# A two-layer graph kernel: the masked attention product in one VectorE instruction from PSUM, and the neighbour maximum in two strided reductions

## The chip, the cores and the metric

The program runs on one core of a Trainium2 chip. The metric is device time in microseconds (us). Three executions of the kernel before gave 5440.72, 5489.24 and 5507.57 us; the median is 5489.24 us. The profile is of one execution, whose span is 5448.3 us.

## The reference, cut to what matters

There are 8 graphs of 2048 nodes with 256 features. Layer 0 takes, for each node, the first 25 neighbours in column order, gathers their 256 features and keeps the maximum per feature; a product with a 512 x 256 matrix, a residual and a layer norm follow. Layer 1 is an attention with 4 heads of 64 features, over the same adjacency matrix.

```python
# layer 0: neighbour maximum
vals, idx = jax.lax.top_k(jnp.where(A != 0, pri, neg_inf), S)       # S = 25, pri = -column
feats = jax.vmap(lambda x, i: x[i])(X, idx)                         # gather 25 rows
agg = jnp.where(valid[..., None], feats, neg_inf).max(axis=2)
out = relu(concat([X, agg]) @ W + b);  x = layernorm(x + out)
# layer 1: attention over the nonzero entries (all are of type 1)
weight = leaky_relu(e_src[i] + e_dst[j], 0.01); weight = where(adj == 0, NEG, weight)
dst = softmax(weight) @ h + bias;  out = per_head_norm(relu(dst) + h);  x = layernorm(x + out)
```

With one edge type, exp(leaky_relu(s + d)) is a factor of i and a factor of j times max(r_i * q_j, 1), where r = exp(0.99 s) and q = exp(0.99 d). The kernel computes that, masks it, and divides by the sum.

## The kernel before, in words

The 16384 nodes are 128 tiles of 128 rows; four tiles are a quad, and `run_quads` unrolls the four steps u = 0 to 3 of a quad. One step works on several tiles at once, each at another stage. Every engine has its own `step` function, and the program order in it is written by hand; engines meet at semaphores.

In step s (= 4q + u) the engines do this:

- **GpSimd (POOL)** gathers the neighbours of tile s: 25 indirect DMAs (L498), one per neighbour slot, each 128 rows of 256 floats into `rows`. It waits for the index list `idx` of that tile, and per chunk of 5 slots until VectorE has read the chunk's old content.
- **VectorE (DVE)** runs the search for tile s+1 in `step`: a chain of 35 links (`LINKS`), each waiting for the one before: the words of the mask (L728, L729), `top32` three times (L715, L717), and the list `idx` at its end (L768). Between the links stands other work at numbered places: the masked units of attention at `UNIT_AT` (and one ahead of the chain, one at the step's end), the residual and norm of tile s-1 at 7 to 17 (L778 at place 7 needs TensorE's product `p_lin`), the maxima of the gathered chunks at 12, 19 and 26 (L836). After the chain come the last maximum, `aggregate` (L845 reduces 5 x 256 to 256, L846 clips and signals `s_agg`), and the last masked unit. In steps with u = 0, `divide` stands at place 6; the rest of a finished quad (`finish_*`) lies in u = 1 to 3.
- **ScalarE (ACT)** makes r*q for each unit (`scaled`, L565: two 128x512 Copy activations with a per-partition scale, from the tile `rb` in SBUF), the mask conversions (L517 to L546), the projection's exponentials (L653 to L663), and the copy of the attention sums out of PSUM (L586).
- **TensorE (PE)** multiplies each masked unit into the accumulators (`attend`, L1231), and does the products and transposes of the two layers. At a step's end it waits for `s_agg`, transposes (L1186), runs `attend` for unit 7, and in the next step comes `back` (u = 0 only) and `product0` (L1199, L1200), which signals `s_lin`.
- **SyncE** issues the plain DMAs. The values r go to DRAM and come back broadcast over 128 partitions into `rb` (1 MB a quad).

Attention of tile block m runs 16 steps behind. A unit is one tile of neighbours j (128) with two heads: before, a step handles 4 neighbour tiles and all four heads, in 8 units. VectorE's unit is one instruction over 2 x 512 elements: max(uv, 1) * mask, both inputs in SBUF (L819). There are four `uv` buffers.

## Time and profile before

| what | value |
|---|---|
| device time, median of 3 (lowest, highest) | 5489.24 us (5440.72, 5507.57) |
| span of the profiled execution | 5448.3 us |
| busy PE / DVE / ACT / POOL | 63% / 76% / 57% / 68% |
| granted TensorE clock, mean | 0.78 of full speed |

For the profiled execution the page gives its span alone, and not the device time around it. Busy shares are means over a start of 16 steps without attention, some 112 steps with everything, and a tail of attention alone. An engine's busy time leaves out the time between its instructions.

### The profile page before, as it was taken

Reading aid. Unit: us, or ns where it says so; the run is one execution under the profiler, and the core shown is the slowest. Engines: PE = TensorE matmul, PEld = TensorE weight load, DVE = VectorE, ACT = ScalarE, POOL = GpSimd, SP = SyncE. Lnnn points to the kernel's source line nnn. Section 1 sums busy time; section 2 is a strip of 40 time slices with the busy share of each in tenths; the row PEclk is TensorE's granted clock in tenths of the full one; section 3 lists DMA queues with packets and bytes.
Section 4 is the critical chain, followed back from the end, with each engine's and each line's share of the span. In section 5 each row is a group of like instructions: output and inputs, shape, how many; then the busy total and the mean of one; then the engine's idle time right before and its main releaser. Section 6 shows DMA issues by size and latency. Waiting matters only on the chain.

```text
span 5448.3 us, 58256 instructions
## 1 busy us (share of the span) xinstructions
PE 3438.2 (63%) x11778; PEld 1438.1 (26%) x11778; DVE 4138.1 (76%) x11484; ACT 3111.4 (57%) x5570; POOL 3717.1 (68%) x3204
## 2 busy tenths in 40 slices
PE   1232467666666767666676666666666666666786
PEld 1121222222222222222222222222222222222222
DVE  4555578878787888878787878888878788787777
ACT  3333456666556666656655655656656666555565
POOL 4666777777777777777777777777777777677400
PEclk9555578777778777878777787787888778778798
DMA  3434344444444444444444444444444444444210
GB/s 113 130 119 136 119 138 128 146 132 146 125 129 133 135 144 135 132 143 129 134 133 133 145 125 127 139 130 146 136 144 131 128 139 131 137 131 133 85 39 27
DMA packets 282021, 692.71 MB, mean 127 GB/s; under 512 B 62849, under 2 KB 130178, under 8 KB 265346
## 3 DMA queue, kind: packets, MB, share of 16 engines
q0 software_dynamic: 153600, 419.64, 26.1%
q1 hardware_dynamic: 128130, 270.41, 15.6%
q14 instruction: 257, 2.11, 0.1%
q8 instruction: 34, 0.56, 0.0%
HBM read 639.21 MB, written 50.59 MB: 127 GB/s over the span
## 4 chain that ended last, share of the span: by engine, by line
POOL 36%; issue 25%; DVE 22%; PE 8%; DMA 4%; ACT 3%; another core or an unknown queue 1%; POOLq 0%; DVEq 0%; SPq 0%; ACTq 0%
POOL rows L498 36%; PE acc L1231 5%; DVE uv L819 5%; DVE rmax L836 4%; DMA rows<-in_x_dram,idx 4%; DVE top L715 2%; DVE key_b L717 1%; PE pB L1199 1%; DVE agg L845 1%; DVE sth L892 1%; ACT uv L565 1%; DVE key_a L717 1%; DVE mvh L898 1%; ACT stage L525 0%
## 5 line engine op out<-in xcount | busy, mean ns | idle before, releaser
L498 POOL DMA_INDIRECT rows<-in_x_dram,idx x3200 | 3716.9, 1162 | 1404.5 <-issue 997.0
L1231 PE MATMUL acc<-uv,hs 128*65 128x512 f32 x4096 | 2301.4, 712 | 707.2 <-DVE uv L819 448.3
L565 ACT ACTIVATE uv<-rb,qj 128x512 f32 (+1 forms) x2048 | 1330.4, 712 | 169.6 <-PE acc L1231 137.6
L819 DVE SCALAR_TENSOR_TENSOR uv<-uv,maskT 128x1024 f32<-128x1024 f32 x1024 | 1239.9, 1221 | 183.6 <-ACT uv L565 148.4
L1231 PEld LDWEIGHTS acc<-uv,hs 128*65 128x65 f32 x4096 | 602.6, 160 | 1992.7 <-issue 1403.4
L836 DVE TENSOR_TENSOR rmax<-rmax,rows 128x1280 f32<-128x1280 f32 x384 | 572.5, 1491 | 600.4 <-DMA rows<-in_x_dram,idx 553.5
L628 ACT ACTIVATE xaT<-pA 128x512 f32<-128x512 f32 x128 | 76.4, 597 | 791.3 <-PE pA L1186 610.6
L542 ACT ACTIVATE stage<-pT 128x1024 bf16<-128x1024 f16 x256 | 260.6, 1018 | 288.8 <-remote 148.0
L1186 PE MATMUL pA<-id,xt 128*128 128x128 f32 x256 | 81.5, 419 | 469.4 <-DVE agg L846 334.2
L640 ACT ACTIVATE x1T<-pA 128x256 f32<-128x256 f32 x128 | 49.2, 384 | 570.8 <-PE pA L1209 394.5
L1199 PE MATMUL pB<-w_sb,xaT 128*128 128x256 f32 x1024 | 348.0, 499 | 18.4 <-ACT xaT L628 8.6
L836 DVE TENSOR_TENSOR rmax<-rows 128x1280 f32<-128x1280 f32 x128 | 191.5, 1496 | 172.6 <-DMA rows<-in_x_dram,idx 172.6
L1199 PEld LDWEIGHTS pB<-w_sb,xaT 128*128 128x128 f32 x1024 | 257.0, 262 | 170.6 <-DVE pad L730 87.6
L845 DVE TENSOR_REDUCE agg<-rmax 128x256 f32<-128x1280 f32 x128 | 297.2, 2322 | 4.4
L1209 PE MATMUL pA<-id,xh 128*128 128x128 f32 x256 | 63.2, 334 | 366.1 <-DVE xh L810 341.5
L546 ACT ACTIVATE maskT<-pT 128x1024 f16 (+1 forms) x256 | 260.5, 1018 | 0.0
L1215 PE MATMUL pB<-wcat,x1T 128*128 128x264 f32 x512 | 205.6, 539 | 81.5 <-ACT x1T L640 63.9
L525 ACT ACTIVATE stage<-adj_sb,minus 128x2048 bf16<-128x2048 int32 x128 | 254.1, 1985 | 0.0
L517 ACT ACTIVATE mask_sb<-adj_sb 128x2048 f16<-128x2048 int32 x128 | 243.0, 1898 | 2.0 <-DMA adj_sb<-in_adj_dram 2.0
L715 DVE MAX8 top<-key_a 128x8 f32<-128x104 f32 (+1 forms) x768 | 209.9, 273 | 34.7 <-DVE key_a L717 10.1
L715 DVE MAX8 top<-key_b 128x8 f32<-128x104 f32 (+1 forms) x768 | 207.5, 270 | 35.5 <-remote 20.6
L1160 PE MATMUL pB<-pack,stage 128*128 128x8 bf16 x2048 | 75.3, 169 | 222.6 <-ACT stage L542 221.2
(113 smaller groups left out, 3755.5 us busy)
## 6 DMA issues: line engine op xcount, KB each, us to landing
adj_sb<-in_adj_dram SPq DMA_DIRECT2D x128, 1024.0 KB
rows<-in_x_dram,idx POOLq DMA_INDIRECT x3200
xh_dram<-xh SPq DMA_DIRECT2D x128, 256.0 KB
rb<-r_dram SPq DMA_DIRECT2D x32, 1024.0 KB
xr<-xh_dram SPq DMA_DIRECT2D x64, 512.0 KB
xt<-in_x_dram SPq DMA_DIRECT2D x128, 128.0 KB
out_dram<-xr SPq DMA_DIRECT2D x32, 512.0 KB
r_dram<-er SPq DMA_DIRECT2D x128, 2.0 KB
```

The source lines that it names most:

```text
L498: nc.gpsimd.indirect_dma_start(rows[:, c, r * C:(r + 1) * C], None, x_rows, bass.IndirectOffsetOnAxis(ap=idx[p][:, k:k + 1], axis=0)).then ...
L517: nc.scalar.activation(mask_sb[:], adj_sb[:], ACT.Sign, accum_out=degree[:, bass.ds(g, 1)]).then_inc(s_mask, 1)
L525: nc.scalar.activation(stage[:].rearrange("p j i -> p (j i)"), adj_sb[:], ACT.Square, scale=2.0, bias=minus1[:], accum_out=adj_sq[:, bass. ...
L542: nc.scalar.activation(stage[:, hf * HALF:(hf + 1) * HALF, :], src, ACT.Square).then_inc(s_stage, 1)
L546: nc.scalar.activation(maskT[:, bass.ds(qg % RING * JT + hf * HALF, HALF), ug * P:(ug + 1) * P], src, ACT.Square).then_inc(s_ring, 1)
L565: last = nc.scalar.activation(uv[k][:, i, :], rb[:, bass.ds(qa % 2, 1), h, :].rearrange("p a i -> p (a i)"), ACT.Copy, scale=q_j(h))
L715: ch.then(nc.vector.max(top[:, k:k + 8], a))
L819: nc.vector.scalar_tensor_tensor(uv[k][:], uv[k][:], 1.0, m, ALU.max, ALU.mult).then_inc(s_u, 1)
L836: nc.vector.tensor_tensor(rmax[:], before, rows[:, c, :], ALU.max).then_inc(s_rfree, 2 if c == 1 else 1)
L845: ch.then(nc.vector.tensor_reduce(agg[:], rmax[:].rearrange("p (r f) -> p f r", f=C), axis=AX.X, op=ALU.max))
L1199: nc.tensor.matmul(p_lin, xaT[:, c, :], w0_sb[:, c, :], start=(c == 0), stop=False)
L1231: last = nc.tensor.matmul(acc[h][0:HW, :], hs[:, (1 - quad.par) * JT + jt, h, :], uv[k][:, i, :], start=(jt == 0), stop=(jt == JT - 1))
```

## The change

Attention is reordered within a quad. Heads are handled in pairs: steps u = 0, 1 do heads 0 and 1 over all 16 neighbour tiles, steps u = 2, 3 heads 2 and 3. The product r*q is no longer formed: the factors are rewritten as mask * max(r, 1/q), with 1/q in `qinv` as the per-partition scalar, and q moved into `hs`. The row r is broadcast over the partitions by TensorE (`broadcast`: two matmuls of `er` with a 0/1 selector, 128x512 each, into the PSUM tiles `rq`), once for each pair, so twice a quad. VectorE then makes each half unit with one instruction over 512 elements, `rq` in PSUM as its first input and the mask in SBUF as its second: 16 a step in place of 8 of 1024. ScalarE's `scaled` goes away, with `r_dram`, `rb` and their DMAs.

Two accumulators in place of four serve a pair, so their hand-over (`numerators` on ScalarE, `back` on TensorE, `divide` on VectorE) happens twice a quad, at u = 0 and at u = 2.

The 25 gathered rows are read in two chunks of 13 and 12 slots. Each chunk is one `tensor_reduce` over a view whose inner dimension steps over the slots (stride 256 floats), at place 19 and at the end of the chain, and `aggregate` joins the two halves with one `tensor_tensor`.

```diff
@@ -44,14 +44,15 @@
 WPT = P // WORD
 NIB = 4
 TOP = 32
-CH = 5
-CR = S // CH
+CH = 2
+SLOTS = (0, 13, S)
 FIRST = S + 1
 HALF = JT // 2
 UNITS = JT * 2
 US = UNITS // QT
+PAIR = 2
+HJ = JT // 2
 UVB = 4
-AHEAD = 3
...
-        rows = sb("rows", [P, CH, CR * C], F32)
-        rmax = sb("rmax", [P, CR * C], F32)
+        rows = sb("rows", [P, S * C], F32)
+        rmax = sb("rmax", [P, CH, C], F32)
...
-        qj = sb("qj", [P, 2 * JT, HEADS], F32)
+        qinv = sb("qinv", [P, 2 * JT, HEADS], F32)
         dj = sb("dj", [P, HEADS], F32)
         wide = sb("wide", [P, HEADS + 1], F32)
-        er = [sb(f"er{p}", [HEADS, P], F32) for p in range(2)]
-        rb = sb("rb", [P, 2, HEADS, IB], F32)
-        uv = [sb(f"uv{k}", [P, 2, IB], F32) for k in range(UVB)]
-        sT = sb("sT", [HW, HEADS, IB], F32)
+        er = sb("er", [P, 2 * N], F32)
+        headsel = sb("headsel", [HEADS, HEADS, P], F32)
+        uv = [sb(f"uv{k}", [P, PAIR, IB], F32) for k in range(UVB)]
+        sT = sb("sT", [HW, PAIR, IB], F32)
+        raw = sb("raw", [P, QT, C], F32)
...
-        acc = [ps(f"acc{i}", [P, 512], F32) for i in range(QT)]
+        acc = [ps(f"acc{i}", [P, 512], F32) for i in range(PAIR)]
+        rq = [ps(f"rq{i}", [P, IB], F32) for i in range(PAIR)]
...
-                    sp.dma_start(r_dram[:, bass.ds((s - 2) * P, P)], er[p][:]).then_inc(s_rst[p], 16)
-                if u == 1 and quad.on(u, QT * BQ - QT):
-                    m = quad.q - BQ + 1
-                    for o in range(2):
-                        for v in quad.reach(lambda q: 32 * (q - BQ + 2)):
-                            sp.wait_ge(s_rst[o], v)
-                            sp.sem_inc(s_go["sp"], 1)
-                    for v in quad.reach(lambda q: UNITS * (q - BQ)):
-                        sp.wait_ge(s_v, v)
-                        sp.sem_inc(s_go["sp"], 1)
-                    dst_rb = rb[:, bass.ds(m % 2, 1), :, :].rearrange("p a h i -> p (a h) i")
-                    src_rb = r_dram[:, bass.ds(m * IB, IB)].partition_broadcast(P)
-                    sp.dma_start(dst_rb, src_rb).then_inc(s_rb, 16)
...
-                    for r in range(CR):
-                        k = c * CR + r
+                    for k in range(SLOTS[c], SLOTS[c + 1]):
                         nc.gpsimd.indirect_dma_start(
-                            rows[:, c, r * C:(r + 1) * C], None, x_rows,
+                            rows[:, k * C:(k + 1) * C], None, x_rows,
...
-                last.then_inc(s_v, 1)
-            def scaled_units(quad, u, a, b):
-                if quad.on(u, QT * BQ):
-                    for n in range(a, b):
-                        scaled(quad, u, n)
+                for v in quad.reach(lambda q: 2 * (q - lag) + pair):
+                    act.wait_ge(s_back, v)
+                for i in range(PAIR):
+                    last = nc.scalar.activation(sT[:, i, :], acc[i][0:HW, :], ACT.Identity, bias=tiny[0:HW, :])
+                last.then_inc(s_sT, 1)
...
-                nc.scalar.activation(dj[:], p_ed, ACT.Exp, scale=LEAK).then_inc(s_ed, 1)
-                nc.scalar.activation(qj[:, bass.ds(t, 1), :], p_ed.unsqueeze(1), ACT.Exp, scale=1.0 - LEAK)
-                nc.scalar.activation(er[p][:], p_es, ACT.Exp, scale=1.0 - LEAK, accum_out=r_sum[:, bass.ds(QT * qg + ug, 1)])
+                nc.scalar.activation(dj[:], p_ed, ACT.Exp).then_inc(s_ed, 1)
+                nc.scalar.activation(qinv[:, bass.ds(t, 1), :], p_ed.unsqueeze(1), ACT.Exp, scale=LEAK - 1.0)
+                nc.scalar.activation(er[0:HEADS, bass.ds(t * P, P)], p_es, ACT.Exp, scale=1.0 - LEAK,
+                                     accum_out=r_sum[:, bass.ds(QT * qg + ug, 1)])
...
-            def masked(quad, u, n):
-                jt, k = QT * u + n // 2, n % UVB
-                for v in quad.reach(lambda q: UNITS * (q - BQ) + US * u + n + 1):
-                    dve.wait_ge(s_v, v)
-                m = maskT[:, bass.ds((quad.q - BQ) % RING * JT + jt, 1), :].to_broadcast([P, 2, IB])
-                nc.vector.scalar_tensor_tensor(uv[k][:], uv[k][:], 1.0, m, ALU.max, ALU.mult).then_inc(s_u, 1)
-                if u == QT - 1 and n == US - 1:
-                    nc.vector.memset(tick[:, 4:5], 0.0).then_inc(s_blk, 1)
+            def masked(quad, u, n, i):
+                pair, jt, k = u // 2, HJ * (u % 2) + n, n % UVB
+                h = PAIR * pair + i
+                if i == 0:
+                    for v in quad.reach(lambda q: UNITS * (q - BQ) + US * u + n - UVB + 1):
+                        dve.wait_ge(s_pe, v)
+                    if n == 0:
+                        dve.wait_ge(s_proj, projected(quad, u))
+                        if u % 2 == 0:
+                            for v in quad.reach(lambda q: 2 * (q - BQ) + pair + 1):
+                                dve.wait_ge(s_rq, v)
+                m = maskT[:, bass.ds((quad.q - BQ) % RING * JT + jt, 1), :].rearrange("p a i -> p (a i)")
+                inv = qinv[:, (1 - quad.par) * JT + jt, h:h + 1]
+                stt = nc.vector.scalar_tensor_tensor(uv[k][:, i, :], rq[i][:], inv, m, ALU.max, ALU.mult)
+                if i == PAIR - 1:
+                    stt.then_inc(s_u, 1)
+                    if u == QT - 1 and n == US - 1:
+                        nc.vector.memset(tick[:, 4:5], 0.0).then_inc(s_blk, 1)
             def maximum(quad, u, c):
-                if c == 1:
-                    for v in quad.reach(lambda q: 16 * CR * (QT * q + u + 1)):
-                        dve.wait_ge(s_rows[0], v)
-                else:
-                    for v in quad.reach(lambda q: CH * (QT * q + u + 1) + c):
-                        dve.wait_ge(s_rfree, v)
-                for v in quad.reach(lambda q: 16 * CR * (QT * q + u + 1)):
+                count = SLOTS[c + 1] - SLOTS[c]
+                for v in quad.reach(lambda q: 16 * count * (QT * q + u + 1)):
                     dve.wait_ge(s_rows[c], v)
-                before = rows[:, 0, :] if c == 1 else rmax[:]
-                nc.vector.tensor_tensor(rmax[:], before, rows[:, c, :], ALU.max).then_inc(s_rfree, 2 if c == 1 else 1)
+                slots = rows[:, SLOTS[c] * C:SLOTS[c + 1] * C].rearrange("p (s f) -> p f s", f=C)
+                nc.vector.tensor_reduce(rmax[:, c, :], slots, axis=AX.X, op=ALU.max).then_inc(s_rfree, 1)
             def aggregate(quad, u):
@@ -842,26 +795,27 @@
                 for v in quad.reach(lambda q: QT * q + u):
                     dve.wait_ge(s_xaT, v)
                 ch = Chain(dve, s_maxc)
-                ch.then(nc.vector.tensor_reduce(agg[:], rmax[:].rearrange("p (r f) -> p f r", f=C), axis=AX.X, op=ALU.max))
+                ch.then(nc.vector.tensor_tensor(agg[:], rmax[:, 0, :], rmax[:, 1, :], ALU.max))
                 nc.vector.tensor_scalar(agg[:], agg[:], lim[u % 2][:, 0:1], lim[u % 2][:, 1:2], ALU.max, ALU.min).then_inc(s_agg, 1)
                 ch.end()
-            def divide(quad):
-                for v in quad.reach(lambda q: q - BQ):
+            def divide(quad, pair):
...
+                        dve.wait_ge(s_out, v)
+                    nc.vector.tensor_tensor(dst[:], raw[:], per_column(bias_b), ALU.add).then_inc(s_fin, 1)
...
-            UNIT_AT = (2, 4, 6, 14, 22, 31)
-            CHUNK_AT = (12, 19, 26)
+            UNIT_AT = (3, 4, 5, 6, 9, 13, 14, 18, 21, 22, 23, 25, 28, 30, 31, 33)
+            CHUNK_AT = 19
...
-                        masked(quad, u, 1 + UNIT_AT.index(place))
+                        masked(quad, u, UNIT_AT.index(place) // PAIR, UNIT_AT.index(place) % PAIR)
                     if behind and place in RESIDUAL_AT:
                         residual(quad, u, RESIDUAL_AT.index(place))
                     if fin and u == 0 and place == DIVIDE_AT:
-                        divide(quad)
+                        divide(quad, 1)
+                    if att and u == 2 and place == DIVIDE_AT:
+                        divide(quad, 0)
                     if behind and place in NORM_AT:
                         norm0(quad, u, NORM_AT.index(place))
-                    if gather and place in CHUNK_AT:
-                        maximum(quad, u, 1 + CHUNK_AT.index(place))
+                    if gather and place == CHUNK_AT:
+                        maximum(quad, u, 0)
...
+            def broadcast(quad, pair):
+                for v in quad.reach(lambda q: UNITS * (q - BQ) + pair * UNITS // 2):
+                    pe.wait_ge(s_u, v)
+                    pe.sem_inc(s_go["pe"], 1)
+                block = (quad.q - BQ) % BQ * IB
+                for i in range(PAIR):
+                    last = nc.tensor.matmul(rq[i][:], headsel[:, PAIR * pair + i, :],
+                                            er[0:HEADS, bass.ds((1 - quad.par) * N + block, IB)], start=True, stop=True)
+                last.then_inc(s_rq, 1)
...
             def step(quad, u):
+                if quad.on(u, QT * BQ):
+                    pe.wait_ge(s_proj, projected(quad, u))
+                    if u % 2 == 0:
+                        broadcast(quad, u // 2)
                 if u == 0 and quad.on(u, FIN):
-                    back(quad)
+                    back(quad, 1)
+                if u == 2 and quad.on(u, QT * BQ):
+                    back(quad, 0)
                 if quad.on(u, 1):
                     product0(quad, u)
-                if quad.on(u, QT * BQ):
-                    if u == 0:
-                        for v in quad.reach(lambda q: q - BQ):
-                            pe.wait_ge(s_accfree, v)
-                    pe.wait_ge(s_proj, projected(quad, u))
+                if quad.on(u, QT * BQ) and u % 2 == 0:
+                    for v in quad.reach(lambda q: 2 * (q - BQ) + u // 2):
+                        pe.wait_ge(s_accfree, v)
                 attend(quad, u, 0, 4)
```

TensorE's order at a step's start moves as follows. These rows are of the kernel before, from the unit that follows the transposes of `agg` at the end of step u = 1 to the first units of step u = 2.

```order
L1186 MATMUL pA<-id,agg 128x128 x2
L1228 REGISTER_ALU
L1231 MATMUL acc<-uv,hs 65x512 x2
L1199 MATMUL pB<-w_sb,xaT 128x256 x4
L1200 MATMUL pB<-b_sb,ones_row 128x256
L1228 REGISTER_ALU
L1231 MATMUL acc<-uv,hs 65x512 x2
```

The same place in the changed kernel:

```order
L1155 MATMUL pA<-id,agg 128x128 x2
L1197 REGISTER_ALU
L1200 MATMUL acc<-uv,hs 65x512 x2
L1138 MATMUL rq<-er,headsel 128x512 x2
L1123 REGISTER_ALU
L1127 MATMUL acc<-id,sT 128x65 x8
L1168 MATMUL pB<-w_sb,xaT 128x256 x4
L1169 MATMUL pB<-b_sb,ones_row 128x256
```

The broadcast and eight transposes now stand between the last unit of a pair and the product that signals `s_lin`.

VectorE in the changed kernel, in step u = 1, from the first masked half unit (place 3 of the chain) to the residual at place 7:

```order
L777 SCALAR_TENSOR_TENSOR uv<-rq,qinv,maskT 128x512
L666 MATCH_REPLACE key_b<-top,key_a 128x128
L777 SCALAR_TENSOR_TENSOR uv<-rq,qinv,maskT 128x512
L664 MAX top<-key_b 128x8
L768 REGISTER_ALU
L777 ISA
L777 SCALAR_TENSOR_TENSOR uv<-rq,qinv,maskT 128x512
L666 MATCH_REPLACE key_a<-top,key_b 128x128
L777 SCALAR_TENSOR_TENSOR uv<-rq,qinv,maskT 128x512
L664 MAX top<-key_a 128x8
L727 SCALAR_TENSOR_TENSOR r<-pB,xt 128x256
```

Between `agg` and this residual there now lie these four half units; before, five whole units lay there (unit 7 of the step that ends, unit 0, and units 1 to 3 at places 2, 4 and 6).

## Rows read from the trace of the kernel before

**Rows 1.** Windows: busy us (instructions) per engine, granted TensorE clock, DMA share, GB/s.
```profile
200.00:600.00 400.00, 127.28 (x592) 80.27 (x593) 208.69 (x691) 142.21 (x275) 270.77 (x266) 0.55 0.41 126
1200.00:4800.00 3600.00, 2419.47 (x8261) 998.05 (x8262) 2885.28 (x8038) 2177.51 (x3912) 2661.96 (x2245) 0.79 0.44 134
```

**Rows 2.** Waits: engine, line, whom it waited for; total us, times, longest.
```profile
DVE rmax L836 <- DMA rows<-in_x_dram,idx: 726.1, 339, 11.1
...
POOL rows L498 <- DVE idx L768: 407.5, 84, 43.0
...
DVE uv L819 <- ACT uv L565: 148.4, 154, 6.5
```

**Rows 3.** Timeline at a step's end: start, length, engine, line, operation [idle before].
```profile
2405.32 1.49 DVE L836 TENSOR_TENSOR rmax<-rmax,rows 128x1280 f32<-128x1280 f32 x1 [1.40 <-DMA rows<-in_x_dram,idx]
2406.07 1.56 POOL L498 DMA_INDIRECT rows<-in_x_dram,idx  x1 [0.30 <-issue]
2406.84 2.31 DVE L845 TENSOR_REDUCE agg<-rmax 128x256 f32<-128x1280 f32 x1
2407.93 0.95 POOL L498 DMA_INDIRECT rows<-in_x_dram,idx  x1 [0.30 <-issue]
```

**Rows 4.** Groups by form: busy us, mean ns of one, idle before and releaser.
```profile
L498 POOL DMA_INDIRECT rows<-in_x_dram,idx x3200 | 3716.9, 1162 | 1404.5 <-issue 997.0 <-DVE idx L768 407.5
...
L819 DVE SCALAR_TENSOR_TENSOR uv<-uv,maskT 128x1024 f32<-128x1024 f32 x1024 | 1239.9, 1221 | 183.6 <-ACT uv L565 148.4 <-issue 33.6 <-DVE dst L926 0.6
...
L836 DVE TENSOR_TENSOR rmax<-rmax,rows 128x1280 f32<-128x1280 f32 x384 | 572.5, 1491 | 600.4 <-DMA rows<-in_x_dram,idx 553.5 <-issue 45.2
...
L845 DVE TENSOR_REDUCE agg<-rmax 128x256 f32<-128x1280 f32 x128 | 297.2, 2322 | 4.4
...
L586 ACT ACTIVATE sT<-acc,tiny 65x512 f32<-65x512 f32 x128 | 77.1, 679 | 25.0 <-PE acc L1231 20.9 <-issue 3.9
...
L778 DVE SCALAR_TENSOR_TENSOR r<-pB,xt 128x256 f32<-128x256 f32 x128 | 52.9, 414 | 97.7 <-PE pB L1200 56.6 <-issue 20.6 <-remote 20.1
L846 DVE TENSOR_SCALAR agg<-agg,lim 128x256 f32<-128x256 f32 x128 | 52.7, 412 | 4.7
```

**Rows 5.** Line L705, the start's four reductions: shortest, median, longest ns.
```profile
L705 DVE TENSOR_REDUCE wcat<-r x4: 419/420/421, 18.4 to 21.2; 128x4 f32<-128x256 f32 x4
```

**Rows 6.** Timeline of VectorE, links of the search with a masked unit between.
```profile
2459.42 0.28 DVE L717 MATCH_REPLACE8 key_b<-top,key_a 128x128 f32<-128x128 f32 x1
2459.61 1.22 DVE L819 SCALAR_TENSOR_TENSOR uv<-uv,maskT 128x1024 f32<-128x1024 f32 x1
2460.75 0.29 DVE L715 MAX8 top<-key_b 128x8 f32<-128x128 f32 x1
2461.07 0.09 DVE L717 MATCH_VALUE_LOAD key_a<-top,key_b 128x8 f32 x1
```

**Rows 7.** Timeline of VectorE and TensorE from the step's end to place 7.
```profile
2454.18 0.41 DVE L846 TENSOR_SCALAR agg<-agg,lim 128x256 f32<-128x256 f32 x1
...
2454.90 0.66 PE L1186 MATMUL pA<-id,xt 128*128 128x128 f32 x2 [9.54 <-issue]
...
2455.78 3.19 PE L1231 MATMUL acc<-uv,hs 128*65 128x512 f32 x4
...
2461.10 0.69 PE L1200 MATMUL pB<-b_sb,ones_row 1*128 1x256 f32 x2
...
2463.05 0.42 DVE L778 SCALAR_TENSOR_TENSOR r<-pB,xt 128x256 f32<-128x256 f32 x1 [0.28 <-PE pB L1200]
```

**Rows 8.** Windows around the same step's end, columns as in Rows 1.
```profile
2450.00:2455.00 5.00, 0.10 (x1) 0.13 (x2) 4.63 (x4) 0.00 (x0) 4.09 (x4) 0.50 0.66 231
...
2460.00:2465.00 5.00, 5.00 (x16) 2.14 (x15) 4.61 (x17) 3.61 (x4) 3.87 (x4) 1.00 0.26 79
```

**Rows 9.** Timeline of TensorE: one unit at either clock.
```profile
2477.58 1.93 PE L1231 MATMUL acc<-uv,hs 128*65 128x512 f32 x4 [0.70 <-issue]
...
2490.63 3.67 PE L1231 MATMUL acc<-uv,hs 128*65 128x512 f32 x4
```

More of the change, by code:

```diff
@@ L298, in layers_program @@
         s_xhst = [sem(f"s_xhst{p}") for p in range(2)]
-        s_rst = [sem(f"s_rst{p}") for p in range(2)]
         s_x1T = sem("s_x1T")
@@ L628, in step @@
                     nc.scalar.activation(xaT[:, :, :], pA[:, :].rearrange("p (c i) -> p c i", c=4), ACT.Copy).then_inc(s_xaE, 1)
-                if next_attends:
-                    for n in range(1, AHEAD):
-                        scaled(quad, u, n, 1)
             def project(quad, u):
@@ L879, in finish_heads @@
                 if part == 0:
-                    nc.vector.tensor_tensor(dst[:], dst[:], per_column(bias_b), ALU.add).then_inc(s_fin, 1)
+                    for v in quad.reach(lambda q: q - BQ - 1):
+                        dve.wait_ge(s_out, v)
+                    nc.vector.tensor_tensor(dst[:], raw[:], per_column(bias_b), ALU.add).then_inc(s_fin, 1)
                 if part == 1:
@@ L1008, in step @@
                     aggregate(quad, u)
-                if att:
-                    masked(quad, u, US - 1)
                 if fin and u == QT - 1:
@@ L1224, in attend @@
                 for n in range(a, b):
-                    jt, hh, k = QT * u + n // 2, n % 2, n % UVB
+                    pair, jt, k = u // 2, HJ * (u % 2) + n, n % UVB
                     for v in quad.reach(lambda q: UNITS * (q - BQ) + US * u + n + 1):
                         pe.wait_ge(s_u, v)
-                    for i in range(2):
-                        h = 2 * hh + i
-                        last = nc.tensor.matmul(acc[h][0:HW, :], hs[:, (1 - quad.par) * JT + jt, h, :], uv[k][:, i, :],
+                    for i in range(PAIR):
+                        h = PAIR * pair + i
+                        last = nc.tensor.matmul(acc[i][0:HW, :], hs[:, (1 - quad.par) * JT + jt, h, :], uv[k][:, i, :],
                                                 start=(jt == 0), stop=(jt == JT - 1))
```

95 lines of the change are left out of this document (33 added, 62 removed).

## The prediction

> **What bounds the kernel now.** I read the windows first, to get the length of a step, then the waits, then the timeline of one step's end. In the middle stretch GpSimd issues 2245 gathers in 3600 us; at 25 a tile that is 89.8 steps of 40.1 us [rows 1]. At the start, without attention, it is 266 gathers in 400 us, or 37.6 us a step. GpSimd alone needs 25 x (1.162 + 0.302 between two) = 36.6 us a step, and 407.5 / 128 = 3.2 us more for the index list [rows 2, 4]. VectorE waits 726.1 / 128 = 5.7 us a step for gathered rows and 148.4 / 112 = 1.3 us for ScalarE [rows 2]; the rest, 40.1 - 5.7 - 1.3 = 33.1 us, is its own chain. So the gathers pace the kernel, closely followed by VectorE, which also holds back the list that the gathers need.
>
> A gather costs 0.95 us when VectorE is in a one-input instruction (the reduction of L845) and 1.56 us when it starts beside a two-input one from SBUF (L836) [rows 3]. The mean of 1.162 [rows 4] is a mixture of the two. The change takes away the two kinds of instruction that do most of this: the masked units and the maxima. GpSimd's step would fall to about 25 x (0.95 + 0.30) + 1.2 for the turn to a new list = 32.5 us. After the change VectorE is therefore the engine to count, and every wait of its own counts in full.
>
> **Masked units.** A unit of 1024 elements lasts 1.22 us but adds less inside the chain: from L717 at 2459.42 to the next link at 2460.75 is 1.33 us, where a link without filler takes its own 0.28 + 0.03, so a unit adds 1.02 [rows 6]; 0.19 us of it overlaps. Six stand there, two outside add some 1.15: 8.4 us a step. A half unit of 512 elements reads PSUM. The nearest row is L778, 256 elements, one input in PSUM, 0.414 us [rows 4]; the slope between L819 and L836 is 0.27 us for 256 elements, so 0.68 us for 512, and 0.49 added. Sixteen make 7.8 us: **-0.6 us a step**.
>
> L778 reads PSUM and takes 414 ns, L846 reads SBUF only and takes 412 [rows 4]: no surcharge shows. The Trainium skill, page "VectorE: DVE Perf Modes", section on the TRN2 errata, gives a fixed part of 120 cycles from PSUM against 58 from SBUF, 65 ns more an instruction; by it sixteen would cost 1.0 us a step more, and the sum would come out 116 us longer. The rows disagree with it here, and I go by the rows.
>
> **The maximum.** Before: three of L836 in the chain at 1.49 - 0.19, one outside at 1.52, L845 at 2.35: 7.8 us a step [rows 4]. After: two reductions over 3328 and 3072 elements and one joint of 256 (0.44, as L846 with its hand-over). Their price is the largest unknown. L845 takes 2.32 us for 1280 elements with an inner step of 1 KB; at the plain 1.05 ns an element and 0.15 us fixed it would be 1.49. L705 shows that plain price, without a stride: 0.42 us for 256 [rows 5]. The surplus of 0.83 us can go two ways. Per element: 1.70 ns each, so 5.8 + 5.4 us. Per output (256, at 3.2 ns): 4.5 + 4.2 us. L705 has 4 outputs and can't tell. Below, the bound is the plain price, 3.6 + 3.4; above, nothing in the trace excludes twice the plain price, 2.1 ns, 7.1 + 6.6. I take the price per element: the stride is what sets L845 apart from L705 and the other instructions, and it is there for each element. So 11.4 in place of 7.8: **+3.6 us a step**; per output it is +1.1.
>
> The Trainium skill, "Advanced Engine Details and Errata", section "SBUF Cachelines", says that accesses which each go to another 16-byte line pay a penalty. L845 agrees with that as far as it goes, since it is slower than its plain price, and this rule speaks against the change.
>
> **Divide.** It happens twice a quad on half the columns: +0.1 us a step (an estimate; a few fixed parts more). VectorE's own chain is then 33.1 - 0.6 + 3.6 + 0.1 = 36.2 us.
>
> **New waits behind the step's end.** VectorE signals `s_agg` at 2454.6; TensorE transposes from 2454.90, runs unit 7 from 2455.78 for 3.19 us, and `s_lin` comes at about 2461.8, 7.3 us or somewhat more after the signal [rows 7]. TensorE is at half clock then: 0.50 before it starts, 1.00 only from 2460 [rows 8]. Before, VectorE filled this time with five units (5.4 us) and 2.4 us of search, and waited 0.28 us at L778. Now it has four half units, 2.0 us, so it arrives after 4.4 us. In steps u = 1 and 3 that is a wait of about 3.2 us at place 7.
>
> At u = 2 the first half unit, at place 3, needs the broadcast, which is queued on TensorE behind the transposes of `agg` and unit 7. These end about 4.6 us after `s_agg`, and two matmul pairs of a unit's size take 1.9 to 3.7 us [rows 9], say 2.7 while the clock rises. The row is there at 7.3, VectorE at 1.1: a wait of 6.2 us. The two copies of ScalarE (L586, 2 x 0.68 [rows 4]) run beside the broadcast; eight transposes and the product follow while VectorE does its half units and the divide, so place 7 adds nothing. At u = 0 `finish_rows`, four instructions of L846's size, covers 1.6 of it: 4.6 us. Mean over a quad: (3.2 + 3.2 + 6.2 + 4.6) / 4 = **4.3 us a step**. The scalar work removed from ScalarE and the DMAs of `rb` had cost the path only the 1.3 us already taken out.
>
> **Sum.** Middle: 36.2 + 4.3 = 40.5 against 40.1 us, x 112 = +45 us. Rows no longer make VectorE wait: the last of 25 gathers is issued 32.5 us after the list and needed at 40. Start: gathers pace it, 37.6 falls to 33.0 (0.5 kept for the small two-input instructions that remain), x 16 = -74 us. Tail: one hand-over more for each of four quads (2 x 0.68 on ScalarE, transposes, divide, some 3.5 us): +14 us. Together -15, so a span of 5433 us. The profiled span, 5448.3, lies 0.7% under the median of 5489.24, and the page gives no device time for this execution; scaled by 1.0075 the forecast is **5475 us**, no change that can be told. About 2% is what a measurement of this kernel can tell from no change.
>
> **Rivals.**
> - *Price per output.* The reductions cost 2.5 us a step less; 38.0 us a step, span 5153, time 5192. For it: L845's groups are short, so a cost for each start of a group is as good a reading. Against it: nothing but the stride. Chance 0.30.
> - *TensorE stays slow after the signal (slower side).* Half units are spread over the step, so TensorE is never long in dense work, and the clock may stay at 0.50 through the unit, the broadcast and the product. A unit then takes 3.67 us, the broadcast 3.7, and the product's second half twice as long [rows 9]: waits grow by 1.9 to 2.4 at odd steps and 1.5 at even ones, 2.0 a step. Span 5433 + 224 = 5657, time 5700. It decides from some 1.1 us a step on, which is half of that. Against it: the same stretch now holds more TensorE work without a gap, and 2460 to 2465 shows it reaching 1.00 after 5 us of work [rows 8]. Chance 0.14.
> - *The reduction costs twice the plain price.* 2.5 us a step more, time up to 5755. Chance 0.08.
> - *The waits don't come.* If TensorE is at full clock when `s_agg` arrives, a unit takes 1.93 us in place of 3.19 [rows 9] and the waits shrink to under 2 us a step: 38.0 a step, about 5190 us. Chance 0.06; the 9.54 us of idle time ahead of these transposes [rows 7] speak against it.
> - *The gathers are not relieved*, because a PSUM input leaves the mask in SBUF. Then GpSimd needs 36.6 + 1.2 us a step, still under 40.5: only the start's 74 us are lost, which stays within the forecast's own range of 5380 to 5590.
>
> The forecast has 0.42. Faster by over 2% (under 5380): 0.30 + 0.04 + a small part of the forecast, 0.36. Slower by over 2% (over 5599): most of the two slow rivals and a little of the forecast, 0.22. Within: 0.42. A range of 5165 to 5650 leaves out the deeper half of the fast cases and the worse half of the slow ones.
>
> **What would show it.** Gathers: mean near 0.97 us, with VectorE waits for rows near zero after the start. Reductions: L789 at 5.8 and 5.4 us (per element), 4.5 and 4.2 (per output). Half units at 0.68 us. New idle time of VectorE ahead of L777 released by TensorE's `rq` matmul, twice a quad, near 6 and 4.6 us, and ahead of the residual near 3 us in odd steps. GpSimd idle, waiting for the list, 7 us a step. The prediction is wrong if the reductions are at the lower price, if the clock behind `s_agg` differs, or if VectorE waits at a place I don't name, such as the free `uv` buffers.

## The result: 30% slower, and the profile after

The changed kernel takes 7097.95 us (median of 4; 7077.05 to 7111.82) against 5472.44 (5440.72 to 5507.57) in the same session: ratio **1.296**, 95% interval 1.288 to 1.304. The forecast was 5475 us, no change that can be told, its range 5165 to 5650. The kernel is clearly slower instead.

First the windows of the changed kernel, of the start and of the middle, columns as in [rows 1]:

```profile
200.00:600.00 400.00, 123.63 (x586) 78.87 (x587) 240.51 (x646) 140.94 (x267) 244.30 (x258) 0.53 0.39 121
1200.00:4800.00 3600.00, 1956.81 (x6118) 765.24 (x6117) 2378.70 (x6373) 935.24 (x1788) 1562.03 (x1629) 0.73 0.31 93
```

1629 gathers are 65.2 steps of 55.2 us, where 40.5 was forecast and 40.1 was measured before [rows 1]. VectorE works 2378.70 / 65.2 = 36.5 us of such a step, GpSimd 24. Neither paces it by its work. The start, without attention, got no faster either: 38.8 us a step, against 37.6 before and a forecast of 33.0.

The groups by form, as in [rows 4], have most of the durations as they were forecast:

```profile
L480 POOL DMA_INDIRECT rows<-in_x_dram,idx x3200 | 3059.9, 956 | 3710.1 <-DVE idx L717 2746.4 <-issue 963.7
...
L777 DVE SCALAR_TENSOR_TENSOR uv<-rq,qinv,maskT 128x512 f32<-128x512 f32 x2048 | 1502.8, 741 | 358.8 <-PE rq L1138 147.6 <-issue 120.6 <-remote 74.5
L789 DVE TENSOR_REDUCE rmax<-rows 128x256 f32<-128x3328 f32 x128 | 739.2, 5775 | 15.9 <-DMA rows<-in_x_dram,idx 15.7
L789 DVE TENSOR_REDUCE rmax<-rows 128x256 f32<-128x3072 f32 x128 | 682.4, 5331 | 3.0 <-DMA rows<-in_x_dram,idx 2.9 <-issue 0.2
...
L727 DVE SCALAR_TENSOR_TENSOR r<-pB,xt 128x256 f32<-128x256 f32 x128 | 54.3, 424 | 918.4 <-remote 732.7 <-issue 103.3 <-PE pB L1169 82.4
```

The reductions cost their price per element, 5.8 and 5.3 us. Gathers fell from 1162 to 956 ns. Rows hardly make VectorE wait: 18.5 us in all, against 726.1 [rows 2]. What is new is the idle time ahead of L727, the residual that needs TensorE's product `p_lin`: 918.4 us in place of 97.7. The waits say more:

```profile
POOL rows L480 <- DVE idx L717: 2746.4, 127, 43.6
...
DVE r L727 <- remote: 732.7, 79, 17.2
...
DVE rden L813 <- remote: 388.4, 40, 16.9
...
DVE top L664 <- remote: 154.8, 98, 3.9
DVE uv L777 <- PE rq L1138: 147.6, 31, 7.6
...
DVE key_a L666 <- remote: 82.0, 42, 2.8
DVE uv L777 <- remote: 74.5, 5, 19.0
DVE key_b L666 <- remote: 60.9, 36, 2.5
```

"remote" stands where the profile finds no instruction of this core whose end fits the release. On a program of one core there is no other core, so it says that the signal came at a time when nobody had just finished. All such waits of VectorE add up to 1536 us, against 64 us before. The time lost against the forecast span is 7107.6 - 5433 = 1675 us, so most of the miss is in this one name; it is not an exact account, since some of these waits would have been there in part without the delay (the forecast itself had 4.3 us of waits a step). GpSimd's 2746.4 us for the list follow from it: the list is late because VectorE is.

The timeline of one step u = 2 shows a case (TensorE, VectorE and the last gathers of the burst):

```profile
2972.86 0.41 DVE L799 TENSOR_SCALAR agg<-agg,lim 128x256 f32<-128x256 f32 x1
...
2977.78 2.17 PE L1138 MATMUL rq<-er,headsel 4*128 x4
...
2979.99 0.75 DVE L777 SCALAR_TENSOR_TENSOR uv<-rq,qinv,maskT 128x512 f32<-128x512 f32 x1 [5.87 <-PE rq L1138]
...
2982.31 0.69 PE L1169 MATMUL pB<-b_sb,ones_row 1*128 1x256 f32 x2
...
2987.06 0.29 DVE L664 MAX8 top<-key_a 128x8 f32<-128x128 f32 x1 [0.17 <-DVE raw L816]
...
2987.25 5.92 PE L1200 MATMUL acc<-uv,hs 128*65 128x512 f32 x8 [4.25 <-issue]
...
2996.68 0.94 POOL L480 DMA_INDIRECT rows<-in_x_dram,idx  x1 [0.30 <-issue]
2997.92 0.94 POOL L480 DMA_INDIRECT rows<-in_x_dram,idx  x1 [0.30 <-issue]
3003.12 0.42 DVE L727 SCALAR_TENSOR_TENSOR r<-pB,xt 128x256 f32<-128x256 f32 x1 [15.76 <-remote]
...
3006.94 3.68 PE L1200 MATMUL acc<-uv,hs 128*65 128x512 f32 x4 [13.77 <-DVE uv L777]
```

The first wait, 5.87 us for the broadcast, is the one forecast (6.2). Then the product ends at 2983.00. In the program L727 waits for one semaphore only, `s_lin`, which this product signals. VectorE is ready for it from about 2987.4, when the link at L664 is done, and starts it at 3003.12: 20.1 us after the product's end and 15.76 us after its own last work. The end of a matmul is modelled in the profile, but TensorE runs eight more matmuls from 2987.25 to 2993.17, in order behind the product, so the product is done long before 3003. Meanwhile GpSimd issues gathers every 1.25 us without a gap, from 2967.93 to 2998.86, and L727 starts 4.3 us after the last. The windows of that stretch:

```profile
2995.00:3000.00 5.00, 0.00 (x0) 0.00 (x0) 0.00 (x0) 0.00 (x0) 2.95 (x4) 0.53 0.39 108
3000.00:3005.00 5.00, 0.00 (x0) 0.00 (x0) 1.88 (x8) 0.00 (x0) 0.00 (x0) 0.50 0.02 6
```

In the first of the two stretches nothing runs on the compute engines but four gathers. Bandwidth is no explanation for the end of the wait: from 3000 on the DMA share is 0.02, and the signal is out until 3003.

In the next odd step the product ends earlier in the burst of gathers, at 3042.36 beside the tenth of them, which is 12.2 us into the burst and not 15.1, and it is handed over as forecast:

```profile
3035.04 0.45 DVE L799 TENSOR_SCALAR agg<-agg,lim 128x256 f32<-128x256 f32 x1
...
3041.67 0.69 PE L1169 MATMUL pB<-b_sb,ones_row 1*128 1x256 f32 x2
3042.61 0.42 DVE L727 SCALAR_TENSOR_TENSOR r<-pB,xt 128x256 f32<-128x256 f32 x1 [2.72 <-PE pB L1169]
```

VectorE waited 2.72 us, where 3.2 was the estimate, and started 0.25 us after the product's end.

The trace also records when a semaphore is updated, though not every time. These records, each set against the nearest earlier end of an instruction that signals the same semaphore, give the delay for the whole run, up to the last gather. Of TensorE's 1639 records 399 came more than 1.5 us late; of ScalarE's 1229, none. For `s_lin` it is 84 of 105, and in 54 of these the update came after the last gather of a burst, in the median 4.3 us after its end. The delay depends on how far the burst has got: of TensorE's signals due beside gathers 1 to 9, 13 of 203 were late, beside gathers 18 to 25, 220 of 225. In the kernel before it was 102 of 1466 in all.

### The profile page after: what moved, and what is told of

Same layout as the page of the kernel before. It is cut to its first block, busy times and chain, and to the rows that moved or that the text cites. A ratio compares the mean times of both kernels' runs of the same rounds, so it can differ in the third digit from the quotient of the medians.

```text
span 7107.6 us, 53875 instructions
## 1 busy us (share of the span) xinstructions
PE 3801.9 (53%) x12034; PEld 1525.5 (21%) x12034; DVE 4705.6 (66%) x12541; ACT 1840.9 (26%) x3522; POOL 3060.1 (43%) x3204
## 4 chain that ended last, share of the span: by engine, by line
DVE 46%; another core or an unknown queue 23%; issue 16%; PE 11%; ACT 2%; DVEq 1%; POOL 0%; ACTq 0%; DMA 0%; POOLq 0%
DVE rmax L789 15%; DVE uv L777 11%; PE acc L1200 6%; DVE top L664 3%; DVE key_b L666 3%; DVE key_a L666 1%; PE rq L1138 1%; PE pB L1168 1%; DVE sth L849 1%; DVE raw L816 1%; PE pA L1155 1%; ACT maskT L528 1%; DVE r L727 1%; DVE xh L759 1%
## 5 line engine op out<-in xcount | busy, mean ns | idle before, releaser
L480 POOL DMA_INDIRECT rows<-in_x_dram,idx x3200 | 3059.9, 956 | 3710.1 <-DVE idx L717 2746.4
L1200 PE MATMUL acc<-uv,hs 128*65 128x512 f32 x4096 | 2557.4, 773 | 1951.5 <-DVE uv L777 932.8
L777 DVE SCALAR_TENSOR_TENSOR uv<-rq,qinv,maskT 128x512 f32<-128x512 f32 x2048 | 1502.8, 741 | 358.8 <-PE rq L1138 147.6
L789 DVE TENSOR_REDUCE rmax<-rows 128x256 f32<-128x3328 f32 (+1 forms) x256 | 1421.6, 5553 | 18.9 <-DMA rows<-in_x_dram,idx 18.5
L1200 PEld LDWEIGHTS acc<-uv,hs 128*65 128x65 f32 x4096 | 655.0, 175 | 3454.6 <-issue 1798.7
L727 DVE SCALAR_TENSOR_TENSOR r<-pB,xt 128x256 f32<-128x256 f32 x128 | 54.3, 424 | 918.4 <-remote 732.7
L556 ACT ACTIVATE sd<-mv,eps 128x1 f32<-128x1 f32 x128 | 37.6, 294 | 1829.7 <-DVE tick L740 1263.0
L813 DVE RECIPROCAL rden<-acc 128x2 f32<-128x2 f32 x256 | 23.5, 154 | 430.6 <-remote 388.4
L664 DVE MAX8 top<-key_b 128x8 f32<-128x104 f32 (+1 forms) x768 | 207.6, 270 | 137.4 <-remote 103.6
L1184 PE MATMUL pB<-wcat,x1T 128*128 128x264 f32 x512 | 190.8, 506 | 196.0 <-ACT x1T L588 181.3
L664 DVE MAX8 top<-key_a 128x8 f32<-128x104 f32 (+1 forms) x768 | 208.0, 271 | 102.0 <-remote 51.3
L666 DVE MATCH_REPLACE8 key_b<-top,key_a 128x104 f32<-128x104 f32 (+1 forms) x768 | 198.9, 259 | 0.0
```

The source lines that it names most:

```text
L480: nc.gpsimd.indirect_dma_start(rows[:, k * C:(k + 1) * C], None, x_rows, bass.IndirectOffsetOnAxis(ap=idx[p][:, k:k + 1], axis=0)).then_in ...
L664: ch.then(nc.vector.max(top[:, k:k + 8], a))
L666: ch.then(nc.vector.match_replace(b, top[:, k:k + 8], a, 0.0))
L777: stt = nc.vector.scalar_tensor_tensor(uv[k][:, i, :], rq[i][:], inv, m, ALU.max, ALU.mult)
L789: nc.vector.tensor_reduce(rmax[:, c, :], slots, axis=AX.X, op=ALU.max).then_inc(s_rfree, 1)
L1184: nc.tensor.matmul(p_h, x1T[:, c, :], wcat[:, c, :], start=(c == 0), stop=(c == 1))
```

## The experiments

Each ratio below is against the kernel before in the same session (5411.14 us for e1 to e4, 5451.37 for e5 to e8, 5425.58 for e9 to e12). The sessions used different chips, so a difference in us between two of them is good to some 60 us.

**Theory G** (gathers' pace): when GpSimd issues gathers without interruption every 1.25 us, the completion signals of TensorE, and to a lesser degree VectorE's, are held back and arrive when the burst is over. Before the change, VectorE's instructions with two inputs in SBUF stretched the gathers ([rows 3]) and kept the pace below that. **Theory H** (hand-over): the new order on TensorE, broadcast and `back` ahead of the product, makes the stall, whatever GpSimd does.

### e1 and e2: each half of the change alone

e1 is the changed kernel with the five-chunk maxima of before; e2 is the kernel before with the two strided reductions.

```diff
# e1, against the changed kernel            # e2, against the kernel before: the reverse
-CH = 2
-SLOTS = (0, 13, S)
+CH = 5
+CR = S // CH
...
-                nc.vector.tensor_reduce(rmax[:, c, :], slots, axis=AX.X, op=ALU.max).then_inc(s_rfree, 1)
+                nc.vector.tensor_tensor(rmax[:], before, rows[:, c, :], ALU.max).then_inc(s_rfree, 2 if c == 1 else 1)
```

Expected of e1:

> Alone the attention part of the change: half units from PSUM, broadcast, hand-over per pair; the maxima are as before (five chunks, four two-input instructions at places 12, 19, 26 and the end, then the short reduction). What is open: in the changed kernel TensorE's semaphore for s_lin reaches VectorE up to 20 us after the matmul, from about the tenth gather of an unbroken row of gathers to 4 us after the last (L727 idle 732.7 us, released by something that the profile does not name). Theory G (gathers at full pace, 1.25 us each without a break, hold back the completion signals of TensorE): the two-input maxima in SBUF slow some gathers again, but the masked units no longer do, so most rows stay at 0.95 us; the stalls stay in part, step near 45 to 50 us, 5900 to 6600 us. Theory H (the new hand-over or the broadcast itself makes TensorE late): the stalls stay in full, 6700 us or more. If the stalls came only with the long reductions: near 5400 us.

Expected of e2:

> Alone the maximum part: two strided reductions of 3328 and 3072 elements, everything else as before (units of 1024 with both inputs in SBUF, ScalarE's products, rb by DMA). VectorE's own chain grows by 3.6 us a step to 36.7 and the waits for rows mostly go; theory G says that the two-input units keep slowing the gathers, so that no long stall of TensorE's signals appears: 37 to 40 us a step, 5350 to 5550 us. Theory H says the same, since there is no new hand-over. If the long one-input reductions were the cause of the stall, this kernel would be above 6300 us.

e1 took 6389.99 us, ratio 1.180 (1.175 to 1.186); e2 5625.13, ratio 1.041 (1.032 to 1.049). Each half leaves one kind of two-input instruction in place, and each has part of the stalls. Waits of e1, then of e2:

```profile
DVE r L728 <- remote: 707.5, 50, 19.3
DVE rmax L797 <- DMA rows<-in_x_dram,idx: 209.7, 106, 10.9
```

```profile
DVE r L777 <- remote: 117.9, 17, 11.0
```

e2 has neither broadcast nor a second hand-over, and stalls at the same residual all the same; that speaks against H. It also speaks against what I had expected under G, no long stall and at most 5550 us: bursts of which only some gathers are stretched still bring some stalls. Side by side, the mean of a gather, the sum of VectorE's remote waits, TensorE's late signals (over 1.5 us, of those recorded), and the time:

| kernel | gather, ns | remote, us | late signals | device time, us |
|---|---|---|---|---|
| before | 1162 | 64 | 102 of 1466 | 5472 |
| e2, reductions only | 1062 | 330 | 135 of 1246 | 5625 |
| e1, masked product only | 1017 | 973 | 384 of 1619 | 6390 |
| both | 956 | 1536 | 399 of 1639 | 7098 |

The faster the gathers, the more stalls. The table orders the cases but does not prove a cause, since other things change with it.

### e3: the changed kernel, each gather followed by a short pause

```diff
                             bass.IndirectOffsetOnAxis(ap=idx[p][:, k:k + 1], axis=0)).then_inc(s_rows[c], 16)
+                        nc.gpsimd.memset(idle[:], 0.0).then_inc(s_idle, 1)
+                        pool.wait_ge(s_idle, k + 1)
+                pool.sem_clear(s_idle)
```

> The changed kernel with one GpSimd memset of 64 elements, waited for, behind each of the 25 gathers: nothing of the work changes, only the pace of the gathers, from 1.25 us to an estimated 1.45 to 1.7 us. Theory G: the completion signals come through, the idle time of L727 and L813 without a named releaser falls from 1121 us to under 200, a step takes 40 to 43 us, 5450 to 5800 us. Theory H: no change or a little slower, 7050 to 7300 us.

The memset writes 64 elements. Measured: **5590.65 us**, ratio 1.031 (1.025 to 1.036), where the changed kernel had 1.296. More work for GpSimd makes the kernel 1507 us faster. Its timeline at the same place, u = 2:

```profile
3032.65 0.17 POOL L485 MEMSET idle<- 128x64 f32 x1
3033.09 0.95 POOL L482 DMA_INDIRECT rows<-in_x_dram,idx  x1 [0.27 <-POOL idle L485]
3034.04 0.17 POOL L485 MEMSET idle<- 128x64 f32 x1
3034.46 3.78 PE L1143 MATMUL rq<-er,headsel 4*128 x4
3034.48 0.95 POOL L482 DMA_INDIRECT rows<-in_x_dram,idx  x1 [0.27 <-POOL idle L485]
...
3038.28 0.75 DVE L782 SCALAR_TENSOR_TENSOR uv<-rq,qinv,maskT 128x512 f32<-128x512 f32 x1 [7.47 <-PE rq L1143]
...
3042.61 0.69 PE L1174 MATMUL pB<-b_sb,ones_row 1*128 1x256 f32 x2
...
3043.34 0.42 DVE L732 SCALAR_TENSOR_TENSOR r<-pB,xt 128x256 f32<-128x256 f32 x1
```

The product ends at 3043.30 and the residual starts at 3043.34: 0.04 us in place of 20.1, with the same order on TensorE, the same broadcast, the same hand-over. (VectorE comes to the residual just then, so the signal was there at the latest 0.04 us after the product.) Over the run 28 of TensorE's 1617 recorded signals are late, none by more than 3.5 us. The gathers now follow each other every 1.39 us instead of 1.25. In the middle stretch the kernel is almost the one forecast:

```profile
1200.00:4800.00 3600.00, 2421.57 (x8184) 984.39 (x8184) 3147.21 (x8487) 1252.49 (x2394) 2488.97 (x4350) 0.81 0.41 124
```

Half of GpSimd's 4350 are memsets, so 2175 gathers, 87 steps of 41.4 us (forecast 40.5). H is refuted: the hand-over is unchanged and its stalls are gone. What stands is that GpSimd's pace of gathers makes them; by which path, no run shows.

### e4 and e5: where the pauses must be

e4 has the memset behind gathers 8 and 16 only, five waited ones of 512 elements, which put 2.8 us more between two gathers each time. e5 has e3's single memset behind gathers 5, 10, 15 and 20.

```diff
+                        if k in (7, 15):        # e5: (4, 9, 14, 19), one memset of 64 elements
+                            for i in range(5):
+                                nc.gpsimd.memset(idle[:], 0.0).then_inc(s_idle, 1)
+                                pool.wait_ge(s_idle, 5 * (7, 15).index(k) + i + 1)
+                pool.sem_clear(s_idle)
```

> The changed kernel with two pauses of about 3 us in GpSimd's row of 25 gathers, behind the 8th and the 16th (five memsets of 512 elements, each waited for); between them the pace stays 1.25 us. Theory G in the form that a backlog builds up over some ten gathers and drains in a break of 3 to 4 us: the stalls go, 5500 to 5800 us. If only the mean pace counts and a break of 3 us drains little: 6300 to 6900 us. Theory H: about 7100 us.

> The changed kernel with the short waited memset of e3 only behind gathers 5, 10, 15 and 20, not behind each: 0.14 us more at four of 25, so the mean pace goes from 1.25 to about 1.27 us a gather. Theory G, pace: what counts is the rate over a burst. The rate is almost as before, so most of the stalls stay: between 6800 us (a fifth of what e3 gained) and 7100 us. Rival B, break: what helped in e3 is that GpSimd waits for something at all, whatever the length, so that four breaks split the burst into runs of five, too short for a stall: 5550 to 5750 us, and 'remote' no longer heads VectorE's waits.

e4 took 5764.98 us, ratio 1.064 (1.059 to 1.069), and its largest remote wait of VectorE is a total of 19.0 us at L671. TensorE's late signals are 114 of 1518, about the share of the kernel before; 25 waits of ScalarE for them make 189.3 us at L531. e5 took 6894.44, ratio 1.264 (1.258 to 1.270), and keeps the stalls:

```profile
DVE r L734 <- remote: 662.4, 70, 18.0
```

So it is not the waiting as such that helps: TensorE's late signals are 391 of 1637 in e5. Runs of eight gathers at full pace do little harm if 2.8 us follow; pauses of 0.14 us at every fifth gather do nearly nothing, about the share of e3's gain that their number gives (4/25 of 1507 is 241, and 204 were gained, across two sessions). The pauses of a burst add up to about 0.5 us in e5, 3.5 in e3 and 5.7 in e4, so these runs fit a limit on how much GpSimd issues over a burst; they do not separate the sum of the pauses from their places.

### e9: the first eight gathers at full pace

```diff
+                        if k >= 8:
+                            nc.gpsimd.memset(idle[:], 0.0).then_inc(s_idle, 1)
+                            pool.wait_ge(s_idle, k + 1 - 8)
+                pool.sem_clear(s_idle)
```

> The changed kernel with e3's waited memset behind gathers 9 to 25 of a tile and none behind the first eight, which run at full pace. In the changed kernel TensorE's signals begin to come late at about the ninth gather of a burst. Theory G, a backlog that builds up over a burst at full pace: eight gathers are too few to build one, so the pause is needed only behind them, and the time is within 100 us of e3's 5590: 5500 to 5700. If the backlog starts with the first gather, part of the stalls comes back: over 5900 us.

5958.00 us, ratio 1.098 (1.093 to 1.103): over 5900, so my version of G with a harmless beginning is wrong. VectorE's waits:

```profile
DVE r L733 <- remote: 422.7, 66, 13.9
```

The first eight gathers add to the delay, although it shows only later: beside gather 10, with the pauses already on, 54 of TensorE's 82 recorded signals are late here, against 0 of 52 in e3. This reads as a backlog that short pauses drain slowly and that a break of e4's 2.8 us behind gather 8 mostly drains (0 of 91 late beside gather 10). The backlog itself was not seen.

### e6 and e7: the pause in kernels whose gathers are stretched anyway

e6 is the kernel before with e3's edit, e7 is e1 with it.

> The kernel before with e3's waited memset behind each gather. Theory G: before, the gathers are stretched to 1.16 us already and few signals come late, so there is nothing to cure; 25 x 0.14 = 3.5 us a step go to the engine that paces it, 40.1 -> 43.3 us a step, 5750 to 5870 us. Rival: the pause helps by something else than the late signals (fewer collisions of gathers with other work), then the kernel before gains as well: under 5450 us.

> The changed kernel's masked product with the maxima of the kernel before (e1), and e3's waited memset behind each gather. Theory G: e3's step of 41.4 us loses the 3.6 us that the strided reductions cost, so VectorE comes to some 37.8 us, and GpSimd to 25 x (1.0 + 0.44) + 1.2 = 37.2: the two nearly tie, 5200 to 5400 us, 1000 us under e1. If the two-input maxima stretch the gathers to 1.06 us as in e2, GpSimd paces at 38.7 and it is 5300 to 5400. Rival, late signals come from the masked product itself whatever the pace: it stays near e1's 6390 us.

e6 took 6215.20 us, ratio 1.140 (1.134 to 1.146); e7 5865.12, ratio 1.076 (1.071 to 1.081). The kernel before gains nothing in time. Its late signals do go, from 102 of 1466 to 0 of 1648, but they had cost it little, and the pause costs more; e7 is 525 us under e1, has no remote wait among VectorE's, and 0 of 1698 late. Both are slower than expected for a plain reason. Groups of GpSimd in e6, then in e7:

```profile
L500 POOL DMA_INDIRECT rows<-in_x_dram,idx x3200 | 3698.7, 1156 | 1628.7 <-POOL idle L503 873.5 <-DVE idx L773 424.7 <-issue 326.3
L503 POOL MEMSET idle<- 128x64 f32 x3200 | 533.5, 167 | 3.0
```

```profile
L483 POOL DMA_INDIRECT rows<-in_x_dram,idx x3200 | 3478.8, 1087 | 1509.2 <-POOL idle L486 801.8 <-issue 451.2 <-DVE idx L723 256.1
```

A gather, its memset and the gaps take 1.156 + 0.167 + (873.5 + 326.3) / 3200 = 1.70 us in e6, 0.24 more than before's 1.46; I had put 0.14. That is 42.5 us a step and GpSimd's alone; 128 x 25 x 0.24 us are 768 us, and e6 lost 764. In e7 the same sum is 1.65 us, 41.1 a step, so the saving on VectorE has nothing to fall on: it waits 922.6 us for rows.

### e8 and e10 to e12: towards a better version

All four have e1's kernel as their base (masked product from PSUM, maxima of before). e8 is e7 with the broadcast for u = 2 moved to the end of step u = 1, and six half units at places 1 to 6. e10 pauses behind gathers 9 to 25 only. e11 has two breaks of five memsets, behind gathers 10 and 18. e12 is e11 with e8's move of the broadcast alone:

```diff
-                    if u % 2 == 0:
-                        broadcast(quad, u // 2)
+                    if u == 0:
+                        broadcast(quad, 0)
...
+                if quad.on(u, QT * BQ) and u == 1:
+                    broadcast(quad, 1)
                 if quad.on(u, 0):
                     transpose_xa(quad, u)
```

> e7 with two further moves: at u = 2 TensorE makes the broadcast of rq at the end of the step before, ahead of the transposes of agg, and VectorE's first six half units stand at places 1 to 6 instead of three to six with the last two at 9 and 13. By the prediction's own count the wait of 6.2 us at u = 2 falls to some 3 and the odd steps' 3.2 us to some 2.2: 1.3 us a step of VectorE. If VectorE paces e7 this gives 100 to 150 us; if the gathers do (37.2 us and more a step), under 50 us.

> e7 (masked product from PSUM, maxima of the kernel before) with the waited memset behind gathers 9 to 25 only. In e7 GpSimd set the pace at 43 us a step: 25 gathers of 1.09 us, 0.39 us between two, 0.17 us of memset. Eight pauses less give GpSimd 8 x 0.25 = 2 us a step back: 5865 - 230 = 5640 us, if no signals come late; theory G expects 5550 to 5700. If late signals return, above 5865.

> The same kernel as e7 with two breaks of five short waited memsets, about 1.5 us each, behind gathers 10 and 18, in place of the 25. GpSimd then needs 25 x (1.05 + 0.30) + 3.0 + 1.2 = 38.0 us a step, VectorE 36.2 - 3.6 + 4.3 = 36.9: if 1.5 us drain the backlog, 38 to 39 us a step and 5200 to 5450 us. If they are too short (e4's were 2.9 us), late signals return and it lies between 5500 and e1's 6390.

> e11 with one move: at u = 2 TensorE makes the broadcast of rq at the end of step u = 1, ahead of the transposes of agg. VectorE's wait of 6 us at place 3 in u = 2 should fall by 3 to 5 us, since only place 7 then waits for the product. Where GpSimd sets the pace, as at 38 us a step, that gives nothing: within 60 us of e11. Where VectorE does, 3 to 5 us a quad, 100 to 150 us less than e11.

| kernel | device time, us | ratio (95%) |
|---|---|---|
| e8 | 5934.25 | 1.088 (1.083 to 1.093) |
| e10 | 5767.18 | 1.066 (1.061 to 1.071) |
| e11 | 5530.48 | 1.020 (1.016 to 1.025) |
| e12 | 5495.46 | 1.013 (1.008 to 1.017) |

e8 loses 69 us to e7: GpSimd paces, and its wait for the list is 391.1 us against 256.1. That the half units put ahead in the search make the list later is my reading; e8 has two moves, and only e12 tests one of them alone. In e10 and e11 late signals are few, but not gone (197.8 us at L734 in e10), and both are above what was expected. e11's two breaks are 1.6 and 1.3 us long, and it lies where it was expected if they were too short. e12's move is worth 35 us, with ranges that overlap slightly, as expected of a kernel that GpSimd paces. None beats the kernel before: in e12 too, VectorE waits 520.9 us for rows. The maxima of before stretch the gathers, and the pauses that replace the stretch elsewhere cost time as well.

## Why the prediction was wrong, step by step

**The step that failed** is the relief of the gathers: "Rows no longer make VectorE wait: the last of 25 gathers is issued 32.5 us after the list and needed at 40." It held for the gathers and the rows (0.956 us a gather, 18.5 us of waits for rows), and I took it as pure gain, in the middle as slack and in the start as -74 us. What the runs showed in its place: bursts at an unbroken 1.25 us hold back TensorE's signals by up to 20 us. It cost 1507 us by e3, which gives 0.14 us of pace back and gets nearly the forecast's kernel. The start is part of it. There e3 takes 36.9 us a step (542 / 2 gathers in 400 us) although GpSimd has 3.5 us more to do in each; less these, 33.4 is left, and 33.0 was forecast, where the changed kernel took 38.8.

The trace of the kernel before had the sign in it, and I did not look for it:

```profile
ACT stage L542 <- remote: 148.0, 37, 9.9
```

ScalarE waits here for TensorE's transposes of the mask, 76.6 of the 148.0 us in the window of the start, where there are no masked units to stretch the gathers. With the pauses of e6 the name is gone from its waits.

**The rivals** all asked what VectorE or TensorE would do with a signal in hand. No rival asked whether signals would travel as before when an engine that is off the path speeds up. The text named "if VectorE waits at a place I don't name" and gave it no price, so the range could not hold it.

**VectorE's chain**, forecast 36.2 us with its gaps; its busy time alone is 36.5, before it was 2885.28 / 89.8 = 32.1 [rows 1]. So +4.4 us a step in place of +3.1.
- *Reductions*: forecast 5.8 + 5.4, measured 5.775 + 5.331. Right. The rivals "per output" and "twice the plain price" are out.
- *Half units*: forecast 0.68 us, measured 0.741. Sixteen of them cost 1.0 us a step more than forecast: +0.4 in place of -0.6. This is most of the 1.3 us. The measured time is 61 ns over my estimate. The Trainium skill, page "VectorE: DVE Perf Modes", section on the TRN2 errata, gives a fixed part of 120 cycles from PSUM against 58 from SBUF, which is an estimate of 65 ns more. I had weighed that rule and set it aside because L778 and L846 tie [rows 4]. They still tie after the change (L727 424 ns, L799 426); they are two different instructions, though, and their tie does not show that a PSUM source is free. The rule's sum was the better one here. No run has the same half unit with its input in SBUF, so the surcharge fits the number and is not shown apart.

**New waits**: forecast 6.2 us for the broadcast at u = 2, 5.87 and 7.47 in the two timelines above; forecast 3.2 at odd steps, 2.72 above. About right: all waits of e3's VectorE for the broadcast are 245.0 us, 46 of them, so 5.3 each, and for the product 155.3, 52 of them, so 3.0 each. In e3's timeline the granted clock was 0.50, the lower of the two levels, from 3030 to 3040, and the broadcast took 3.78 us, where it took 2.17 above. This is the rival of the slow clock in part, and 1.6 us in that one step: it accounts for 7.47 in place of 5.87.

**Sum without the stall**: e3's middle has 41.4 us a step against 40.5, and its span is 5588.8 against 5433. The half units' 1.0 us is as large as the 0.9, but e3 also waits 192.4 us for rows, which the forecast put at nothing, so how the 0.9 divides is not shown. That the sum comes this close is in part luck. The forecast was a fair account of a kernel that did not come about.

## What to carry to other kernels

An engine that stops being the bound does not only wait: it can run its burst at full pace, and here the others' signals came late for it. Before counting a relief as slack, look in the trace for the longest stretch in which that engine already runs unhindered (here the start), and for how late the others' signals are there. And when a profile shows waits on "remote" in a program of one core, compare the end of the instruction that should have released them with the start of the waiting one: a gap that ends shortly after another engine's burst points to that engine, and a small pause in it is a cheap test.

## What the runs showed of the hardware

- 25 indirect gathers issued every 1.25 us held TensorE's completion signal back 20.1 us, until 4.3 us after the last gather's end. Of TensorE's recorded signals 399 of 1639 were over 1.5 us late, of ScalarE's none of 1229. At 1.39 us a gather it is 28 of 1617; with two breaks of 2.8 us 114 of 1518; with four of 0.14 us 391 of 1637. VectorE's own are late to a lesser degree: its remote waits for its own chain (L664, L666) are at most 3.9 us. On which path the signals wait was not seen.
- A gather is 0.95 us beside VectorE instructions of one SBUF input (L845 [rows 3]) and beside those with the first input in PSUM (L777 in the burst above); the mean was 956 ns with the masked units in PSUM and strided reductions, 1162 with both kinds of two-input instruction.
- A reduction whose inner step is 1 KB costs 1.74 ns an element over 3328 and 3072 elements alike (5775 and 5331 ns); L845's 1280 elements take 2322 ns, 1.81 each.
- 512 elements with one input in PSUM take 741 ns (L777); 256 take 424 (L727), and another instruction of 256 with its input in SBUF takes 426 (L799).
